# A transformer block on one Trainium2 core: the router reads raw rows instead of normalised ones

## The reference, cut to what matters

```python
x = x + tanh(g_xattn[1]) * L1_xattn(layernorm(x), ctx, ...)
y = layernorm(x)                       # (x - mean) / sqrt(var + eps), over the 256 channels
wg_n   = wg / max(norm(wg, axis=1), 1e-4)
logits = (y @ w_red) @ wg_n.T          # 2048 tokens x 8 experts
gates  = softmax(logits, axis=1)
scores, idx = max(gates), argmax(gates)
h = gelu(y @ W1[idx] + b1[idx]);  o = (h @ W2[idx] + b2[idx]) * scores
x = x + tanh(g_ffn[1]) * o
```

## Time and profile before

| what | value |
|---|---|
| median of 3 runs | 493.53 us (493.13 to 494.15) |
| the profiled execution's own time | 495.09 us |
| its span, first to last instruction | 493.3 us |
| PE busy | 439.5 us, 89% of the span |
| DVE / ACT / POOL busy | 337.2 / 257.3 / 127.3 us |
| mean granted clock of TensorE | 0.95 of full speed |
| chain that ended last: PE / DVE / ACT | 59% / 16% / 7% of the span |

### The profile page before, as it was taken

One profiled execution on the slowest core, in us unless ns is written; L12 is line 12 of the kernel. 1 busy time (PEld: TensorE's weight loads), 2 busy tenths in 40 slices (PEclk: granted clock), 3 DMA queues, 4 the chain that ended last, 5 costly groups with the idle time before them and its releaser, 6 DMA issues.

```text
span 493.3 us, 7541 instructions
## 1 busy us (share of the span) xinstructions
PE 439.5 (89%) x2318; PEld 305.2 (62%) x2319; DVE 337.2 (68%) x748; ACT 257.3 (52%) x449; POOL 127.3 (26%) x138
## 2 busy tenths in 40 slices
PE   8999999999974199999999999999868799999991
PEld 7788544444451188887667667775648467676771
DVE  4989973489998999656665976568757255555551
ACT  3564555499999744134756666575630433324210
POOL 6524262000003504211950001000102734543222
PEclk9999999999985589999999999999996999999997
DMA  8900000000020040003990000000053411221000
GB/s 247 249 3 0 3 2 0 0 0 0 0 59 1 0 102 1 0 1 108 391 353 0 1 1 1 1 0 0 1 180 89 104 47 48 69 50 47 16 28 1
DMA packets 27421, 27.20 MB, mean 55 GB/s; under 512 B 11611, under 2 KB 23586, under 8 KB 27139
## 3 DMA queue, kind: packets, MB, share of 16 engines
q1 hardware_dynamic: 25187, 21.73, 13.9%
q0 software_dynamic: 2208, 5.14, 3.6%
HBM read 22.63 MB, written 5.15 MB: 56 GB/s over the span
## 4 chain that ended last, share of the span: by engine, by line
PE 59%; DVE 16%; ACT 7%; issue 4%; POOL 1%; DMA 1%; DVEq 1%; ACTq 0%; POOLq 0%
PE bank L1649 48%; PE bank L1937 4%; PE bank L1693 2%; ACT tmp L901 2%; PE bank L2133 2%; DVE big_g L1372 2%; ACT big_u L750 2%; PE bank L1955 2%; ACT big_u L896 1%; DVE amZ L1282 1%; DVE amP L1346 1%; DVE amU L1288 1%; DVE mx L1465 1%; DVE big_g L1466 1%; DVE big_g L476 1%
## 5 line engine op out<-in xcount | busy, mean ns | idle before, releaser
L1649 PE MATMUL bank<-yT,ffn_w 128*128 (+1 forms) x192 | 83.0, 593 | 0.0
L750 ACT ACTIVATE big_u<-bank 77x512 f32<-77x512 f32 (+3 forms) x102 | 56.3, 584 | 36.8 <-PE bank L1937 24.3
L1649 PEld LDWEIGHTS bank<-yT,ffn_w 128*128 128x128 f32 x192 | 36.2, 190 | 44.8 <-issue 43.1
L1649 PE MATMUL bank<-ffn_w,big_u 128*128 128x256 f32 x192 | 42.6, 380 | 0.9 <-ACT big_u L750 0.9
L1649 PE MATMUL bank<-big_u,yT 128*128 x184 | 42.0, 380 | 1.6 <-DVE yT L1612 1.6
L1649 PE MATMUL bank<-big_g,yT 128*128 x92 | 41.8, 596 | 1.7 <-issue 1.2
L968 ACT ACTIVATE big_g<-big_g 128x308 f32<-128x308 f32 x64 | 29.0, 457 | 26.2 <-DVE big_g L1466 25.7
L1044 ACT ACTIVATE yT<-yT 128x512 f32<-128x512 f32 x23 | 14.5, 630 | 54.0 <-DVE yT L1608 54.0
L1649 PE MATMUL bank<-k_blockdiag,big_g 128*128 128x308 f32 x128 | 40.2, 430 | 2.5 <-DVE big_g L1466 2.1
L1649 PEld LDWEIGHTS bank<-ffn_w,big_u 128*128 128x128 f32 x192 | 36.2, 190 | 6.1 <-ACT big_u L750 1.1
L1649 PEld LDWEIGHTS bank<-big_u,yT 128*128 128x128 f32 x184 | 34.0, 190 | 6.7 <-issue 2.6
(11 more groups left out here) (282 smaller groups left out, 833.1 us busy)
## 6 DMA issues: line engine op xcount, KB each, us to landing
big_g<-in_L_ffn_W SPq DMA_DIRECT2D x1, 4096.0 KB, 13.3
big_u<-in_L_ffn_W SPq DMA_DIRECT2D x1, 4096.0 KB, 24.8
x_rows<-in_x SPq DMA_DIRECT2D x4, 512.0 KB, 6.5
ffn_w<-in_L_ffn_b SPq DMA_DIRECT2D x1, 2048.0 KB, 26.2
tmp<-bias_by_distance SPq DMA_DIRECT2D x2, 616.0 KB, 5.9
token_rows<-x_rows SPq DMA_DIRECT2D x1, 1032.0 KB, 7.4
tmp<-in_L_ffn_b SPq DMA_DIRECT2D x1, 1024.0 KB, 5.5
token_rows<-x_rows SPq DMA_DIRECT2D x1, 774.0 KB, 9.2
```

Of the source, the lines that this page charges most:

```text
L750: act.activation(out_, in_, ACT.Copy, **k).then_inc(done, 1)
L1649: return pe.matmul(out_, lhsT=lhsT, rhs=rhs, start=first, stop=last)
```

## The change

The logits of a token are linear in its normalised row. So the mean can be taken out on the weight's side: subtracting each router weight column's mean over the 256 channels gives the same product from a raw row as from a centred one. The reciprocal deviation is a positive factor of each token, which changes neither the largest expert nor ties. The changed kernel therefore

- centres the transposed `w_red` on ACT while it copies it (a copy that also sums, a scaling by -1/256, an addition),
- transposes raw rows of `X` as soon as `x3_done` says so, and has no `y4` and no `router_in`,
- has POOL reorder the deviations by turn (four small copies) and multiply the logits less their maximum by them (`LXS`), before ACT's exponent,
- moves `ln_rows` of the first 14 tiles in front of the last residuals, and that of the last two behind the choice of the expert,
- has PE and ACT take the transposes in another order.

```diff
+            pool.wait_ge(s.rstd_d, 2)
+            pool.tensor_copy(rstdp[:, 0:TB - NEAR], rstd4[:, NEAR:TB])
+            pool.tensor_copy(rstdp[:, TB - NEAR:TB], rstd4[:, 0:NEAR])
+            pool.tensor_copy(rstdp[:, TB:NT - NEAR], rstd4[:, TB + NEAR:NT])
             rstds_of(TB, TB + NEAR, s.mv_d, s.rstd_d, NT)
+            pool.wait_ge(s.rstd_d, 3)
+            c.link(pool.tensor_copy(rstdp[:, NT - NEAR:NT], rstd4[:, TB:TB + NEAR]))
+            pool.wait_ge(s.lx_sb, 1)
+            pool.tensor_tensor(LXS, LX, rstdp[:, :].unsqueeze(2).to_broadcast([P, NT, E]), ALU.mult).then_inc(s.lxs_sb, 1)
...
-            copy(WRT, pb[6][0:G, 0:D], s.l1_ps, WRT_, s.wrT_sb)
+            act.wait_ge(s.l1_ps, WRT_)
+            c.link(act.activation(WRT, pb[6][0:G, 0:D], ACT.Copy, accum_out=wrm[:, :]))
+            c.link(act.activation(wrm[:, :], wrm[:, :], ACT.Copy, scale=-1.0 / D))
+            act.activation(WRT, WRT, ACT.Identity, bias=wrm[:, 0:1]).then_inc(s.wrT_sb, 1)
...
-            for k in range(1, 4):
+            for k in range(1, 5):
                 y4T_out(k)
             attended(NT - 2)
-            y4T_out(4)
+            y4T_out(5)
             logits_out(0)
             logits_out(1)
-            y4T_out(5)
             y4T_out(6)
+            y4T_out(7)
             logits_out(2)
-            y4T_out(7)
             logits_out(3)
-            act.wait_ge(s.lx_sb, 1)
-            act.activation(EX, LX, ACT.Exp).then_inc(s.ex_sb, 1)
+            act.wait_ge(s.lxs_sb, 1)
+            act.activation(EX, LXS, ACT.Exp).then_inc(s.ex_sb, 1)
...
-            router_in(0, TB)
-            router_in(TB, TB + 2)
             head_out(NT - 2, 0)
             head_out(NT - 2, 1)
-            router_in(TB + 2, NT - NEAR)
+            dve.wait_ge(s.rstd_d, 2)
+            ln_rows(0, TB)
+            ln_rows(TB + NEAR, NT).then_inc(s.ln_row, 1)
             residual(NT - 2, (NB - 1) * TB, 0)
             residual(NT - 2, (NB - 1) * TB, 1)
             moments(NT - 2, (NB - 1) * TB)
-            ln_rows(0, TB)
-            ln_rows(TB + NEAR, NT).then_inc(s.ln_row, 1)
-            router_in(NT - NEAR, NT)
-            ln_rows(TB, TB + NEAR).then_inc(s.ln_row, 1)
...
             dve.tensor_tensor(OHB[:, :, :], OH, LMB, ALU.is_equal).then_inc(s.oh_sb, 1)
+            dve.wait_ge(s.rstd_d, 3)
+            ln_rows(TB, TB + NEAR).then_inc(s.ln_row, 1)
             dve.wait_ge(s.ex_sb, 1)
...
-                    pe.wait_ge(s.y_d, 2 * k + u + 1)
-                    transposed(ps[:, u * D:(u + 1) * D], y4[:, 2 * k + u, :], s.y4T_ps)
+                    pe.wait_ge(s.x3_done, 2 * k + u + 1)
+                    transposed(ps[:, u * D:(u + 1) * D], X[:, tile_at(2 * k + u), 0:D], s.y4T_ps)
...
             y4_in(3)
+            y4_in(4)
             tokens_back(NT - 2)
-            y4_in(4)
+            y4_in(5)
             project_in(NT - 2)
             logits(0)
             project(NT - 2)
             logits(1)
-            y4_in(5)
             y4_in(6)
+            y4_in(7)
+            logits(2)
             logits_back(0)
             logits_back(1)
-            logits(2)
+            logits(3)
             logits_back(2)
-            y4_in(7)
-            logits(3)
             logits_back(3)
```

More of the change, by code:

```diff
@@ L175, in __init__ @@
         self.rstd_d = sem("rstd_d")
-        self.y_d = sem("y_d")
+        self.lxs_sb = sem("lxs_sb")
         self.y4T_ps = sem("y4T_ps")
@@ L407, in flamingo_kernel @@
         WGNT = sb("wgnT", [G, E])
+        wrm = sb("wr_mean", [G, 1])
+        rstdp = sb("rstd_by_turn", [P, NT])
         GM = sb("gm", [P, CH, 32])
@@ L412, in flamingo_kernel @@
         B2 = part(TMP, 0, [P, E * D])
-        y4 = part(TMP, 2048, [P, NT, D])
+        LXS = part(TMP, 2048, [P, NT, E])
         lT = part(BIGG, 11264, [P, 4, P])
@@ L1512, in _ @@
                 pair(b * TB + 2 * FAR, b * TB + TB - 2, b)
-            def router_in(a, b):
-                for p in range(a, b):
-                    t = tile_at(p)
-                    dve.wait_ge(s.rstd_d, 1 if p < TB else 2 if p < NT - NEAR else 3)
-                    dve.tensor_scalar(y4[:, p, :], X[:, t, 0:D], mv4[:, t, 0:1], rstd4[:, t:t + 1],
-                                      ALU.subtract, ALU.mult).then_inc(s.y_d, 1)
             def ln_rows(a, b):
```

## The result

The changed kernel takes 491.19 us (median of 20 runs, 489.83 to 494.64) where the kernel before takes 494.16 us on the same chip (20 runs, 493.13 to 496.24): ratio 0.9941, 95% interval [0.9925, 0.9957], 3.0 us less by the medians. The forecast was 490.9 us, the range 490.1 to 492.4. Two repeats gave 0.9947 [0.9929, 0.9966] and 0.9942 [0.9922, 0.9962].

A forecast was written before the change was run, and what follows sets the result against it. The prediction took PE to set the end for 59% of the span, with a serial router chain. It summed -2.65 + 0.07 = -2.58 us (the +0.47 already included), so 493.53 became 490.9 us, range 490.1 to 492.4.

The forecast's parts named there:

- Four more transposes ahead of `tokens_back`: On PE before the heads' results: four added transposes delay `tokens_back` and the residuals by 0.47 us, with no cover allowed.
- The last pair from the raw residual: Router's last transposes start 2.65 us earlier, less 0.07 for ACT's copies; the maximum comes 2.58 us earlier, at 365.60.
- Coefficient beside the count: POOL's multiplication (0.43 us) and the exponent finish before PE's count, costing 0; at 1.36 us a loss of 0.4 to 0.5.
- The rival that the clock helps the count: PE's count before the row numbers runs at full clock, total 490.6 us; chance 0.06.
- The third store: Last rows' store, issued 1.7 us later, still lands before 375 and costs 0; at 9.0 us it loses 0.2.
- the prediction's own test: The prediction is wrong if POOL's first gather is released by the store instead of by DVE.
- Another of its signs of being wrong: The prediction is wrong if the first expert loops show a granted clock below 1.
- an estimate of 2.6 us for this store alone: From the skill page's fit: the 258 KB third store alone would be down some 2.6 us after issue, so no wait.
- Router weight, first fourteen copies: ACT's centring adds 0.74 to 1.0 us but hides behind PE's wait; removing DVE's first 14 copies gains nothing; both 0.
- The clock in the first expert steps: Rival: PE's clock falls to its low level in the first expert steps, adding 1.2 us, total 492.1; chance 0.10.

The follow-up runs named there:

- wait_rstd: Changed kernel with one wait put back: PE transposes the last pair of tiles only once the last rows' deviation is there; 495.51 us, ratio 0.9994 to the kernel before.
- the third execution: Second unaltered repeat of the changed kernel, beside other kernels on one chip; 492.40 us, ratio 0.9942 to the kernel before.
- rows_early: Changed kernel with the last rows' deviation and mean written ahead of the maximum, so the third store is issued earlier; 493.24 us, ratio 0.9956.
- old_order: Changed kernel with raw rows kept, but PE and ACT in the earlier order of transposes, logits and copies; 492.99 us, ratio 0.9960.
- b2_last: Changed kernel with the load of the second expert bias moved behind the three row stores on SP's queue; run twice, 491.88 and 492.03 us, ratios 0.9928 and 0.9930.
- copies_back: Changed kernel with 14 of DVE's 16 normalising copies put back, their results unread; 492.37 us, ratio 0.9945.
- b2_share: Changed kernel with the bias load behind the row stores and DVE's 128x1104 shares multiply right behind the row numbers; 491.88 us, ratio 0.9935.
- filled: Changed kernel with PE's filler behind the count of rows per expert raised from 11 to 20; 492.63 us, ratio 0.9942.
- share_first: Changed kernel with DVE's 128x1104 multiply that places the shares moved right behind the row numbers; 491.47 us, ratio 0.9928.
- plain_weight: Changed kernel with the router's weight copied but not centred, so other experts are chosen; 490.98 us, ratio 0.9923.

## Why the prediction was right, and where it was not

*Four more transposes ahead of `tokens_back`: +0.47.* Measured +0.39 in the column "heads" (0.39 to 0.44 in all twelve profiles with this order).

*The last pair from the raw residual: 2.65 - 0.07.* This is the step that carried the forecast. The maximum is 2.99 us nearer to the heads' results, less 0.39 is 2.60, against 2.58 forecast. wait_rstd shows the cause: with the one wait back, the last pair starts 2.64 us later, and with the low clock behind it all is lost. What the prediction did not see is how the two parts of the change share it; the order adds more than half once the rows are raw (1.46 of 2.58), because in the old one the transposes back stand ahead of the last pair.

*Coefficient beside the count: 0.* Right: POOL's multiplication took 0.44 us (forecast 0.43), and the exponent was done before DVE asked for it. The rival that the clock helps the count (chance 0.06) came on top: the stage to the row numbers is 10.06 us and not 10.47, so 0.41 us. It holds in most executions, not in the third.

*The third store: 0, bounds 0 and 0.2.* This step failed in the profiled execution, by its argument that the same bytes are queued earlier and are therefore down earlier, before 375. The bias is issued as before, behind the residuals, and the large stores go 1.3 us sooner (362.72 against 364.02). Yet they land 2.4 and 2.2 us later: 11.1 and 12.6 us after their issue, 7.4 and 9.2 before. The bytes took longer, at 243 GB/s and not 335 from 364 to 368 us, and the third store behind them lands at 377.01 and not at 374.8. Its later issue (367.14, 1.38 us later than before) is not the reason, as rows_early, old_order and wait_rstd show. That the stores moved too close behind the bias is how the traces read; no run changes that distance alone, b2_last only takes the bias away from them. The gather starts 1.86 us after the row numbers were begun, where 1.11 were usual: 0.75 us. This exceeds the bound although the bound was too wide for the landing that it assumed: it left out the 0.9 us that POOL needs after the row numbers anyway, so a store down at 376.5 would have cost nothing. And 0.41 us of the 0.75 are the count's gain taken back: in the third execution, without that gain, the store holds nothing.

*What no step named: 0.64 us.* Started 0.54 us inside DVE's multiply, the first gather took 1.93 us and not 1.29. Together the second gather lost 4.09 - 2.71 = 1.38 us. In the two repeats the loss was 0.15 and 0. By the prediction's own test (the gather must not be released by the store) this part was wrong. Another of its signs of being wrong came too, a clock below 1 in the first expert steps; the third, a maximum later than 366, did not.

*The Trainium skill's page "DMA: Bandwidth & Descriptors", section "Anatomy of one DMA — SWDGE (gpsimd) path"*, had led to an estimate of 2.6 us for this store alone. The section's fit is for transfers that GpSimd issues; this one is issued by SP. b2_last shows it with an empty queue ahead of it and the bias 0.4 us behind: 3.4 us (3.2 and 3.6 in the two other such profiles). The measurement decides. So the price of the store in the changed kernel is the queue ahead of it, not the transfer.

*Router weight, first fourteen copies: 0.* copies_back shows the second. For the first, no profile shows a delay: ACT takes 1.23 us where it took 0.36 (0.87 more, forecast 0.74 to 1.0), and PE's wait near 172 us is still ended by DVE, though it is down from 1.89 to 1.07 us.

*The clock in the first expert steps*, a rival with a chance of 0.10, is what seven of the thirteen profiles with some part of the change show in their first group (5.13 to 6.28 us against 3.69), and one in its second. The chance was too low. The price was about right: over the eight profiles with such a group the last stage is 101.6 us in the mean, over the five without one 100.3 (99.51 to 100.81), so 1.3 us, against 1.2. DVE's waits below blur this. (As worked out, the 1.2 was a slip: half of the 1.7 us that it starts from is 0.85.) Whether the kernel before has fewer such executions, its one profile (100.80, without) cannot tell.

*The sum for the profiled execution.* -0.19 (up to 179 us) + 0.39 - 2.99 - 0.41 + 1.38 - 0.05 + 0.14 = -1.73 us to the last store. The runs show 3.0 less; the repeats' profiles lose 0.15 and 0 at the gather and not 1.38. The forecast's 2.58 was right in its mechanism. That the time came so close, 491.19 against 490.9, is in part luck: the helping clock and the held gather, which the sum leaves out, have opposite signs, and a gain larger by 0.4 us met a starting value of 493.53 that is 0.6 us below the median of the 20 runs.

## What to carry to other kernels

Where two engines hand tiles back and forth, a wait that falls frees only the time to the next thing in the in-order queue; the order must be changed with it, and here the order brought the larger half. A step that comes earlier turns whatever it needs from elsewhere into the next wait: look up for each transfer not only when it is issued but what is queued ahead of it, and move what nobody needs yet behind it. The same bytes, queued sooner and closer together, were down later here. Cut profiles at fixed points when whole times spread by more than the effect.

## What the runs showed of the hardware that was not expected

- A gather of GpSimd that starts while VectorE's 128x1104 multiply (f32 to bf16, 1.30 us) runs ends 1.16 to 1.17 us after it: durations 1.44, 1.93, 2.16, 2.24 and 2.38 us in five profiles (b2_share, changed, copies_back, filled, rows_early), 1.29 or 1.30 us in the nine where it starts before or after. The multiply takes 1.29 or 1.30 us in all fourteen.
- One 258 KB store behind 2.8 MB landed 14.0 to 14.7 us after the first of these transfers was issued, in ten profiles, whether it was issued 3.0 or 8.2 us after it; with the 1 MB load moved behind it, it landed in 3.2 to 3.6 us.
- Issuing that store took SyncE 3.08 us when it came 3.0 us after the first transfer, 1.14 to 1.43 us at 3.6 to 4.8 us, and 0.36 us at 6.7 and 8.2 us (old_order, wait_rstd), although 7.4 and 5.9 us were still to go to its landing; 0.36 us also in b2_last.
- While the 1 MB load and the two large stores were under way together, the DMA engines moved 243 GB/s at a share of 0.94 (changed kernel, 364 to 368 us); in b2_last the stores alone moved 336 GB/s at a share of 1.01 (360 to 364 us). Why is open.
- The granted clock fell in the middle of a stretch in which PE was busy with filler, after pauses (filled), and within 2 us of the end of a pause of 2.45 us (wait_rstd).
- VectorE's two waits in the first expert steps, put down to no engine, appear in some executions of one program and not in others. They are 3.12 and 2.87 us before, 5.22 and 0.77 in b2_share, and 5.9 to 6.0 us together in all five profiles that have both. With a first group of 3.7 us, the third expert group starts 15.7 to 15.8 us after the first where both waits occur and the second group is not slow either (four profiles), and 14.6 and 14.7 us after it in the two without them (share_first, plain_weight): they delay it by about 1.2 us. Their cause is open.
